# A graph and mixture-of-experts kernel: ten row loads issued one block later, and a wait between two parts of GpSimd's gathers

## The reference, cut to what matters

```python
h = (x_flat @ W_gat).reshape(M, HEADS, NUM_EXPERTS)
e = leaky_relu(a_src[src] + a_dst[dst])            # per edge, 4 heads
ee = exp(e - segment_max(e, dst)[dst])
alpha = ee / (segment_sum(ee, dst)[dst] + 1e-16)
agg = segment_sum(h[src] * alpha[:, :, None], dst).reshape(M, 16) + b_gat
scores = _layernorm(agg, ln_gamma, ln_beta).reshape(M, HEADS, NUM_EXPERTS).mean(1)
topk_s, topk_i = top_k(scores, 2)
w = softmax(topk_s)
for ei in range(NUM_EXPERTS):
    g = where(topk_i == ei, w, 0.0).sum(-1)
    hh = gelu(x @ W1[ei] + b1[ei])
    out = out + g[..., None] * (hh @ W2[ei] + b2[ei])
```

## Time and profile before

| what | value |
|---|---|
| device time, three runs | 2619.4 us median (2608.82 to 2625.35) |
| the profiled execution's own time | 2620.25 us |
| its span, first to last instruction | 2618.4 us |
| mean granted TensorE clock | 0.839 of full speed |
| busy: PE, DVE, ACT, POOL | 74%, 46%, 34%, 56% of the span |
| granted clock from 2395 us to the end | 0.50 |
| stretch 2409 to 2430 us: DMA | 340 GB/s, engines all but idle |
| stretch 2465 to 2500 us: PE, DVE, POOL busy | 2.92, 10.85, 20.43 of 35.00 us; DMA 18 GB/s |
| stretch 2528 to 2554 us: DVE busy | 22.32 of 26.00 us; DMA 325 GB/s |

### The profile page before, as it was taken

The page is one execution under the profiler, slowest core; times in us unless marked ns, Lnnn a source line. Parts: engine busy times, 40 slices in busy tenths (PEclk is TensorE's granted clock), DMA queues, the critical chain, the costliest instruction groups (busy, mean ns, idle before and its releaser), DMA issues. The chain is left out here.

```text
span 2618.4 us, 26714 instructions
## 1 busy us (share of the span) xinstructions
PE 1939.7 (74%) x7528; PEld 1333.0 (51%) x7528; DVE 1195.3 (46%) x2204; ACT 880.0 (34%) x1904; POOL 1475.7 (56%) x1512
## 2 busy tenths in 40 slices
PE   5698988877777776765547898888978888893236
PEld 4555555554455544443446666555656555562223
DVE  6353323355455554532475654436355141104279
ACT  3433444444434353442324112221312213223024
POOL 2366666666666665666711666666656666662600
PEclk8899999898888888977765899999989988996555
DMA  5443332434444343453357321212212212214754
GB/s 186 142 153 116 88 90 86 118 116 135 120 126 133 110 142 111 129 181 90 99 168 255 121 51 37 72 37 51 58 37 51 58 37 60 51 37 130 229 165 145
DMA packets 197051, 282.87 MB, mean 108 GB/s; under 512 B 43023, under 2 KB 147443, under 8 KB 195762
## 3 DMA queue, kind: packets, MB, share of 16 engines
q0 software_dynamic: 61280, 115.13, 17.6%
q1 hardware_dynamic: 97218, 121.11, 14.1%
q10 hardware_dynamic: 38416, 44.96, 5.2%
HBM read 195.29 MB, written 85.80 MB: 107 GB/s over the span
## 5 line engine op out<-in xcount | busy, mean ns | idle before, releaser
L864 POOL DMA_INDIRECT ag_msg<-xn_tab,step_src x784 | 783.0, 999 | 436.8 <-issue 224.6
L1840 POOL DMA_INDIRECT edge_rows<-hx_d,gat_src x648 | 621.4, 959 | 335.6 <-issue 186.5
L1132 PE MATMUL ag_ps<-ag_msg,ag_hot 128*128 x1760 | 508.6, 439 | 162.2 <-POOLq L850 72.6
L1132 PEld LDWEIGHTS ag_ps<-ag_msg,ag_hot 128*128 128x128 f32 x1760 | 370.3, 219 | 301.5 <-issue 244.0
L886 DVE TENSOR_TENSOR acc<-acc,ag_ps 128x257 f32 x440 | 186.1, 423 | 579.7 <-PE ag_ps L1132 253.0
L2042 PE MATMUL ex_ps<-co_rows 128*128 128x256 f32 x1568 | 390.1, 403 | 65.7 <-issue 56.1
L2025 PE MATMUL ex_ps<-co_rows 128*128 128x448 f32 x896 | 368.6, 566 | 37.4 <-issue 14.2
L2042 PEld LDWEIGHTS ex_ps<-co_rows 128*128 128x128 f32 x1568 | 311.9, 202 | 134.1 <-issue 83.3
L1311 ACT ACTIVATE gat_self<-iota_row,step_nloc 128x128 f32<-128x128 f32 x880 | 270.8, 388 | 316.7 <-remote 120.2
L2025 PEld LDWEIGHTS ex_ps<-co_rows 128*128 128x128 f32 x896 | 175.7, 200 | 208.9 <-issue 192.6
L1954 DVE TENSOR_TENSOR hi_one_low<-hi_numbers,hi_low 128x2048 bf16<-128x2048 f32 x64 | 146.4, 2287 | 236.6 <-remote 220.3
(11 more groups left out here) (387 smaller groups left out, 2032.2 us busy)
## 6 DMA issues: line engine op xcount, KB each, us to landing
y_d<-co_rows ACTq DMA_DIRECT2D x28, 896.0 KB
co_rows<-y_d SPq DMA_DIRECT2D x28, 896.0 KB, 8.3
ag_msg<-xn_tab,step_src POOLq DMA_INDIRECT x784
xnT<-base_d SPq DMA_DIRECT2D x7, 1792.0 KB
edge_rows<-hx_d,gat_src POOLq DMA_INDIRECT x648
base_d<-xnT ACTq DMA_DIRECT2D x7, 1024.0 KB
sums_d<-edge_rows SPq DMA_DIRECT2D x5, 1344.0 KB
xg<-in_x_dram SPq DMA_DIRECT2D x7, 896.0 KB, 6.1
```

The lines of the kernel that those rows point to most:

```text
L864: pool.indirect_dma_start(msg[:, b % RING, u, 0:D], None, c.xn_tab, bass.IndirectOffsetOnAxis(ap=t.idx[:, at:at + 1], axis=0)).then_inc(s_ ...
L1132: last = nc.tensor.matmul(bank[(at + r) % BANKS][:, 0:ROWW], hot[:, k, v0 + r * JOIN + j, :], ring[:, j * ROWW:SLOTS * ROWW][:, ds(places[ ...
L1840: pool.indirect_dma_start(G[:, j % RING, w, :], None, c.hx_d, bass.IndirectOffsetOnAxis(ap=plan.idx[:, at + w:at + w + 1], axis=0)).then_i ...
```

## The change

Two edits. In `gat_gather_experts` SyncE no longer issues `load_rows` for the two early groups, and in `gat_combine` its loop over groups starts at 0 instead of 2. In `gat_combine` GpSimd waits for `s_sel` at 2, that is for TensorE's last lane product, between gather 14 and gather 15.

```diff
@@ gat_gather_experts, block.sync
                     for i in range(2):
                         sp.wait_ge(s_st[i], 16 * len(spans[i::2]))
-                for g in range(len(early)):
-                    c.load_rows(sp, early[g], g)
                 for i in range(2):
                     sp.wait_ge(s_st[i], 16 * len(spans[i:LOW_SPANS:2]))
@@ gat_combine, block.sync
-                for g in range(len(early), GROUPS):
+                for g in range(GROUPS):
                     if g >= NB:
 
                         sp.wait_ge(s_out[g % NB], 16 * (g // NB))
@@ gat_combine, block.gpsimd
                 for t in range(TILES):
+                    if t == FIRST:
+                        pool.wait_ge(s_sel, 2)
                     pool.indirect_dma_start(num[:, t, :], None, c.sums_d,
```

## The result

The changed kernel takes 2590.07 us (median of 4 runs, 2579.0 to 2599.82), the kernel before 2622.38 us in the same comparison (4 runs, 2608.82 to 2627.63). The ratio is 0.9876, 95% interval 0.9843 to 0.9908: 32.3 us between the medians, faster by 0.9 to 1.6%. Forecast were 2590 us and a range of 2578 to 2606. The profiled execution of the changed kernel took 2597.62 us, one of its slower ones.

What follows compares the result with a forecast made beforehand. It took late load issues at the last block's door, then TensorE signals delayed by unbroken gathers, as the bound. Gains of 16.7 and 13.5 us, 30.2 together, off 2620.25 gave 2590 us, range 2578 to 2606.

Steps and rivals of the forecast that it cites:

- T: Moment the last block (gat_combine) opens, from which forecast times count; 2429.86 us before, forecast at 2413.2.
- two outputs over (second L2362): Last block, output(0) and output(1) beside the gathers: delayed, over at T+86, between T+78 and T+92; undisturbed T+66.
- tail: Last block, from 2529.33 to the end, 89.1 us with no gathers: costed at no change.
- Part 1: Door of the last block: ten loads leave the expert block, so it opens 16.7 us earlier.
- V: Mark for comparing the profiles: end of VectorE's last sums in the block before the last.
- Part 2: Last block: GpSimd's wait before gather 15 frees the lane products; gates_of(0) ends at T+38.5 instead of T+72.0.
- the loads are the cause: Rival, last block: loads, not gathers, cause the delay, so only Part 1 gains; 2603.5 us, chance 0.12.
- part 3: Ahead of gates_of(1): gathers (T+78) or delayed outputs (T+86) set its start; gain 13.5 us.
- The other limb, the gathers: Ahead of gates_of(1): from T+32, 35 gathers take 43.8 us and some 2.5 us to land, giving T+78.

Runs made afterwards that it cites:

- after: The changed kernel with both edits, in the first comparison against the kernel before: median 2590.07 us, ratio 0.9876.
- l_after_again: Kernel before with ten loads moved, no GpSimd wait, all last-block loads held until the lane products are done; chip 14, 2590.49 us in one run.
- p1: The changed kernel without GpSimd's wait, so only the ten loads move; chip 4, 2306.61 us, ratio 0.9929 to the kernel before.
- p2: The kernel before with only GpSimd's wait added, loads unmoved; chip 4, 2331.36 us, ratio 1.0049.
- after_again: The changed kernel with both edits, run again on chip 14 against the kernel before: 2568.93 us, ratio 0.9856.
- both_again: The changed kernel with both edits, run on chip 13 against the kernel before: 2317.73 us, ratio 0.998.
- cut3: The changed kernel with three groups (21 tiles) instead of two in the first gates, wait after 21 gathers; chip 14, 2560.48 us, ratio 0.9833.
- before_again: The kernel before, unchanged, profiled again on chip 14: 2610.65 us in one run.
- x6_transposes: The changed kernel with TensorE's gate transposes of groups 0 and 1 done six times over (42 instead of 7 each); chip 13, 2311.29 us in one run.

## Why the prediction was right, and where it was only lucky

| step | forecast | measured (after) |
|---|---|---|
| 1. T moves by | 16.7 us | 16.9 |
| 1. loads start | T+2.5 | T+1.7 |
| 2. L2362 first | T+22 to T+24 | T+20.6 |
| 2. 15th gather | T+32 | T+30.7 |
| 2. gates_of(0) from L2377 | 14.5 us | 13.9 |
| 3. 35 gathers | 43.8 us | 47.9 |
| 3. landing of the last | 2.5 us | 4.9 |
| 3. two outputs over (second L2362) | T+86, between T+78 and T+92; undisturbed T+66 | T+61.0 |
| 3. gain at gates_of(1) | 13.5 us (by L2362) | 18.2 (by L2377) |
| 4. tail | no change | 87.0 against 86.9 |

Part 1 was right in mechanism and size. It holds on all chips: V to T is 4.8 us in each kernel with the loads moved and 21.6 to 21.9 in each without; ScalarE's leftover exponentials set it.

Part 2 was right in mechanism for the lane products: the run of gathers beside them delays TensorE and VectorE, and breaking the run frees them. l_after_again shows that it is the gathers. The forecast gave "the loads are the cause" 0.12; that case is out. Taken as a rule for every long run of gathers it is wrong, as the next paragraph shows.

The step that failed is in part 3: "T+86, between T+78 and T+92" for the second L2362, taken because the outputs would be caught in the delay. They were not; the outputs ended at T+61. The other limb, the gathers (T+78), was under-sized by 5 us: the gathers took 4.1 us longer and landed 2.4 us later, on a 15th gather 1.3 us earlier. So the bound was the gathers at T+83.4 (L2377). Two errors of opposite sign left the gain 4.7 us short. The forecast took 30.2 us off 2620.25; the two profiles differ by 35.1 us from V on, and the medians by 32.3 us, off 2622.38. That these come to within 0.1 us of each other is luck: the runs of the changed kernel lie up to 21 us apart.

The lengthened gathers are visible in the row of 2.09 us above; most take 0.94. Six of the 35 take 1.25 to 2.09 us, 4.35 us in all beyond 0.94 each, and all six stand beside VectorE's L2464, an addition whose two inputs are both in SBUF, the on-chip memory. The one of 2.09 us, which starts while L2464 runs, ends 0.82 us behind it (2473.20 and 2472.38), and L2464 keeps the length that it has without gathers, 2.02 to 2.03 us. Beside the L2467 of 2472.49, as long but with one input in PSUM (TensorE's result memory), the gather of 2473.50 takes its 0.94. The Trainium skill (SBUF — State Buffer, "SBUF: two separate sides") says that a VectorE instruction with two SBUF inputs and a GpSimd instruction that reads SBUF take a shared pair of ports as an exclusive lock: the first to start keeps it for its whole length, and the other blocks. The trace agrees for GpSimd; it shows no VectorE instruction that waited.

The prediction drew from the same section that TensorE never waits on anyone at that memory. On chips 4 and 13 the trace agrees (98 products in one piece beside the gathers). On chip 14 and in the first comparison TensorE is held beside gathers, in one beat with VectorE, and no run here shows by what way, so that statement on the ports is neither borne out nor refuted there.

What the prediction could not know: it took the delay for a property of the kernel. It is one of the kernel on some chips. By the table, the wait would have cost 10 us wherever the kernel before takes 2320 us. Its gain on a slow chip was not measured alone: both p1 and p2 ran on quick chips only. The 18 us behind T in after and after_again are what the wait gives there if moving the loads changes nothing behind T. The quick chips show that it changes nothing (167.5 us behind T in p2, 167.2 in both_again); on the slow one it is argued. The nearest run there, l_after_again, holds the loads back further still, has no wait, and keeps the delay.

Still open: why TensorE and VectorE are delayed beside gathers on one chip and not on another; why the outputs escape it; the parts alone on a slow chip. One candidate has no run against it: each run on record lists its span and its granted clock, so each was being traced, and whether the delay is there without tracing isn't known.

## What to carry to other kernels

The last engine to reach a barrier sets it, and issuing transfers counts as work: beside a queue full of loads ten load issues took 20.65 us here, and moved behind the barrier they cost nothing. Before buying a wait that separates two engines, price what it holds back (here 9.8 us of gathers, paid in full wherever the delay is absent), and look whether the stall that it cures is there on every chip: let the unchanged kernel run beside each trial. When a step frees time in front of a wait, the work behind that wait is the next thing to move forward, as cut3 does.

## What the runs showed of the hardware that I had not expected

The same kernel takes 2605 to 2622 us on one kind of chip and 2321 to 2323 us on another. The mark is in the waits over the whole kernel. ScalarE's waits for the experts' second layer, on chip 14 (before_again) and on chip 13 (both_again):

```profile
ACT co_rows L2108 <- remote: 222.4, 37, 14.1
```

```profile
ACT co_rows L2106 <- PE ex_ps L2040: 296.3, 112, 4.4
```

The row gives us in total, times and the longest. On chip 13 all 112 waits end with TensorE's record and the longest is 4.4 us; on chip 14 37 of the 112 copies wait for a "remote" signal, up to 14.1 us. It looks like the delay of the earlier trace rows, through the whole expert stage. By the pages of the two profiles ScalarE idles 459 us ahead of this line on chip 14 and 296 us on chip 13, 162 us less. GpSimd idles 763 us ahead of its gathers at L864 and L1840 on chip 14 and 504 us at the same gathers on chip 13, 259 us less. The two may overlap in time, so they can't be added; the kernels before differ by 282 us, and that the delay makes up all of them was not tested.

In x6_transposes TensorE's clock rose. Beside the 42 transposes and the bias products behind them (stretch: its length in us, then PE, weight loads, DVE, ACT, POOL busy, then granted clock, DMA share, GB/s):

```profile
2180.00:2184.00 4.00, 4.00 (x21) 2.41 (x19) 3.92 (x11) 0.00 (x0) 3.08 (x4) 0.50 1.10 337
...
2187.60:2190.80 3.20, 3.20 (x15) 2.50 (x16) 0.46 (x1) 3.20 (x9) 2.53 (x3) 1.00 1.11 327
```

```profile
2187.55 3.28 PE L2245 MATMUL co_ps_b<-co_b,lane_hot 4*128 4x256 f32 x14 [0.98 <-ACT lane_hot L2255]
```

The grant went from 0.50 (1.2 GHz) to 1.00 (2.4 GHz) after TensorE had been busy without a gap for the first transposes, and the 14 bias products took 3.28 us instead of 6.34. In both_again the clock stays at 0.50 there. VectorE waited for ScalarE's terms in that place (5.2 us at L2464), so it gained nothing.
